# A graph network and mixture-of-experts kernel on one core: the edge units' first product gets a contraction of 128 rows, the experts' inner features six near-equal pieces

## The reference, cut to what matters

```
hid = silu(edge_length_embedded @ fc_w0 / sqrt(8))      # 8 features -> 64
w = hid @ fc_w1 / sqrt(64)                              # 64 -> 4 x 64 weights of one edge
msg = products of w with h[edge_src] and the edge's 4 attributes
y = segment_sum(msg, edge_dst)
```

```
h = silu(x @ w1[e].T) * (x @ w3[e].T)                   # 256 -> 682
out += gate[e] * (h @ w2[e].T)                          # 682 -> 256
```

## Time and profile before

| what | us |
|---|---|
| median of the runs shown | 4059.72 |
| span of the profiled execution | 4057.3 |
| edge convolution, from its barrier to its node products | 2790.9 to 3432.3 |
| node products and routing | 3432.3 to 3586.5 |
| routed experts, blocks | 3586.5 to about 4021 |
| sum of pairs and store of the output | to 4057.3 |

### The profile page before, as it was taken

One profiled execution on the slowest core, in us unless ns is written; L12 is line 12 of the kernel. 1 busy time (PEld: TensorE's weight loads), 2 busy tenths in 40 slices (PEclk: granted clock), 3 DMA queues, 4 the chain that ended last, 5 costly groups with the idle time before them and its releaser, 6 DMA issues. The chain is left out here.

```text
span 4057.3 us, 61050 instructions
## 1 busy us (share of the span) xinstructions
PE 3711.8 (91%) x18981; PEld 3087.0 (76%) x18981; DVE 2525.8 (62%) x5060; ACT 1533.3 (38%) x3578; POOL 758.0 (19%) x614
## 2 busy tenths in 40 slices
PE   5996879999999999999998799787999999779996
PEld 2554459989899899898997688655888888758884
DVE  7774755555555555555554555544777777577775
ACT  0363211121211211212112544334888886135553
POOL 0000000000000000000000200003888885012221
PEclk9997989999999999999999899898999999779998
DMA  1364112222222222222221211012333332411113
GB/s 41 64 102 87 48 50 78 87 67 85 76 79 86 74 80 87 67 85 76 79 85 40 66 30 31 13 41 61 93 93 93 94 93 68 177 44 35 38 35 116
DMA packets 297743, 288.61 MB, mean 71 GB/s; under 512 B 101485, under 2 KB 272847, under 8 KB 296806
## 3 DMA queue, kind: packets, MB, share of 16 engines
q1 hardware_dynamic: 233867, 208.29, 17.8%
q0 software_dynamic: 56576, 66.41, 6.4%
q10 hardware_dynamic: 7002, 10.15, 0.7%
HBM read 241.89 MB, written 42.47 MB: 70 GB/s over the span
## 5 line engine op out<-in xcount | busy, mean ns | idle before, releaser
L974 PE MATMUL bank<-a_wide,parts 125*128 125x448 f32 x4200 | 871.5, 367 | 0.1
L974 PEld LDWEIGHTS bank<-a_wide,parts 125*128 125x128 f32 x4200 | 785.7, 188 | 77.2 <-issue 10.1
L2205 POOL DMA_INDIRECT rows<-h_dram,src_t x400 | 493.5, 1234 | 124.1 <-DVE prod L2394 87.3
L2321 ACT ACTIVATE hot<-eq,ea 125x80 f32<-125x80 f32 x1600 | 413.2, 350 | 0.0
L949 POOL TENSOR_TENSOR nf_g<-nf,nf_g 128x896 fp32r<-128x896 f32 x42 | 94.5, 2249 | 1525.4 <-ACT nf_g L1112 1525.4
L1024 DVE CAST a_wide<-a_cols 125x2240 fp32r<-125x2240 bf16 x210 | 274.5, 1324 | 156.5 <-PE bank L974 141.0
L983 PE MATMUL bank<-nf_g,whh 128*128 128x448 f32 x1512 | 339.6, 369 | 0.0
L983 PE MATMUL bank<-msg,wc 128*128 128x448 f32 x1512 | 338.9, 368 | 0.0
L2247 PEld LDWEIGHTS bank<-prod,hot 125*80 125x80 f32 x2400 | 294.6, 150 | 54.1 <-issue 0.7
L2247 PE MATMUL bank<-prod,hot 125*80 125x128 f32 x2400 | 327.9, 273 | 0.0
L1117 ACT ACTIVATE msg<-bank 128x448 fp32r<-128x448 f32 x84 | 41.1, 542 | 702.6 <-PE bank L974 702.6
(11 more groups left out here) (431 smaller groups left out, 5894.4 us busy)
## 6 DMA issues: line engine op xcount, KB each, us to landing
a_cols<-a_dram SPq DMA_DIRECT2D x210, 546.9 KB
a_dram<-a_cols SPq DMA_DIRECT2D x15, 1250.0 KB, 10.9
w<-in_w SPq DMA_DIRECT2D x4, 2728.0 KB
deg_bc<-deg_dram SPq DMA_DIRECT2D x42, 224.0 KB, 6.1
gate_bc<-gate_dram SPq DMA_DIRECT2D x42, 224.0 KB, 3.2
rows<-h_dram,src_t POOLq DMA_INDIRECT x400, 4.2
w<-y_rows SPq DMA_DIRECT2D x12, 512.0 KB, 10.1
w<-in_w SPq DMA_DIRECT2D x5, 1024.0 KB
```

The source lines that it names most:

```text
L974: ins = nc.tensor.matmul(p_msg[f][:, 0:GW], parts[0:SPB, m, c * HB + k, f * 128:(f + 1) * 128], a_wide[u % 2][0:SPB, k, :], start=(c == 0 ...
L2205: nc.gpsimd.indirect_dma_start(out=rows[n % ITC][:, :], out_offset=None, in_=h_dram, in_offset=bass.IndirectOffsetOnAxis(ap=src_t[:, n:n + ...
L2321: ins = nc.scalar.activation(hot[:, q % 2, j, m, :], eq[:, q % 2, j, :], ACT.Copy, scale=ea4[:, q * UC + j, m:m + 1])
```

## The change

`ea8` and `fw0` get 128 partitions in place of 24. POOL fills both with zeros once, ahead of the zeros of `acc`; the loads of `ea8` still write 24 rows, and the product L2224 reads all 128. SP waits for the zeros ahead of its first load, DVE ahead of its first write to `fw0`. The 682 inner features are cut into four pieces of 114 and two of 113. The list of pieces also sets the loads of `w2`, the turns, the copies and the products down. DVE's two copies in `turned` become one.

```diff
-HCH = [(k * 128, min(128, HID1 - k * 128)) for k in range((HID1 + 127) // 128)]
+LONG, SHORT = (4, 114), (2, 113)
+HCH = [(k * LONG[1], LONG[1]) for k in range(LONG[0])] + [(LONG[0] * LONG[1] + k * SHORT[1], SHORT[1]) for k in range(SHORT[0])]
...
-        ea8 = sb(ctx, "ea8", [24, 2, UE], F32R)
+        ea8 = sb(ctx, "ea8", [128, 2, UE], F32R)
...
-        fw0 = sb(ctx, "fw0", [24, 128], F32R)
+        fw0 = sb(ctx, "fw0", [128, 128], F32R)
...
+                sp.wait_ge(rest_zero, START + 2)
                 with sp.Fori(0, rounds) as r:
...
-                        sp.dma_start(ea8[:, b, :].bitcast(F32), ea8_dram[:, q * UE:(q + 1) * UE]).then_inc(ea_in[b], 16)
+                        sp.dma_start(ea8[0:24, b, :].bitcast(F32), ea8_dram[:, q * UE:(q + 1) * UE]).then_inc(ea_in[b], 16)
...
             def _(pool):
+                nc.gpsimd.memset(fw0[:, :].bitcast(F32), 0.0).then_inc(rest_zero, 1)
+                nc.gpsimd.memset(ea8[:, :, :].bitcast(F32), 0.0).then_inc(rest_zero, 1)
                 nc.gpsimd.memset(acc[:, :, :], 0.0).then_inc(acc_zero, 1)
...
                 dve.wait_ge(w_split, START + 2)
+                dve.wait_ge(rest_zero, START + 2)
...
-                nc.vector.tensor_tensor(fw0[:, :], fw0_raw[:, :], fw0_high[:, :], ALU.subtract).then_inc(w_split, 1)
+                nc.vector.tensor_tensor(fw0[0:24, :], fw0_raw[:, :], fw0_high[:, :], ALU.subtract).then_inc(w_split, 1)
...
-    IN_0 = 4
+    IN_0 = LONG[0]
...
-                    nc.scalar.activation(g_t[:, 0:IN_0, :], p_g[0][:, 0:IN_0 * 128].rearrange("p (h c) -> p h c", c=128), ACT.Copy)\
+                    nc.scalar.activation(g_t[0:LONG[1], 0:IN_0, :], p_g[0][0:LONG[1], 0:IN_0 * 128].rearrange("p (h c) -> p h c", c=128), ACT.Copy)\
...
-                    o, sz = HCH[-1]
-                    nc.vector.tensor_copy(g_t[:, IN_0:NH - 1, :], p_g[1][:, 0:(NH - 1 - IN_0) * 128].rearrange("p (h c) -> p h c", c=128))
-                    at_h = (NH - 1 - IN_0) * 128
-                    nc.vector.tensor_copy(g_t[0:sz, NH - 1, :], p_g[1][0:sz, at_h:at_h + 128]).then_inc(gt_done, 1)
+                    nc.vector.tensor_copy(g_t[0:SHORT[1], IN_0:NH, :], p_g[1][0:SHORT[1], 0:SHORT[0] * 128].rearrange("p (h c) -> p h c", c=128))\
+                      .then_inc(gt_done, 1)
```

More of the change, by code:

```diff
@@ L2121, in edge_convolution @@
     src_t, rel0, base_row, rounds_t, iota_w = tables
-    (w_in, w_split, silu_done, hid_high, scaled, acc_zero, tab, ea_in_a, ea_in_b, hid_mm, hid_done, w_mm, eq_done, hot_done, p_done, sum_mm, sum_copied, turned, added,
+    (w_in, w_split, silu_done, hid_high, scaled, rest_zero, acc_zero, tab, ea_in_a, ea_in_b, hid_mm, hid_done, w_mm, eq_done, hot_done, p_done, sum_mm, sum_copied, turned, added,
      u_mm, mix_mm, t_done, b_done, x_done, stat_done, passed, *gathered) = sems(*("c_" + s for s in (
-         "w_in w_split silu hid_high scaled acc_zero tab ea_in_a ea_in_b hid_mm hid w_mm eq hot prod sum_mm sum_copied turned added "
+         "w_in w_split silu hid_high scaled rest_zero acc_zero tab ea_in_a ea_in_b hid_mm hid w_mm eq hot prod sum_mm sum_copied turned added "
          "u_mm mix_mm t b x stat passed").split()),
```

## The result

The changed kernel takes 4134.9 us (median of 4 runs, 4130.7 to 4137.5), the kernel before 4059.4 beside it (4056.9 to 4059.7): 1.019 times, 95% interval 1.0175 to 1.0204. It is slower, as forecast, but by 75 us where 42 were forecast, and outside the range.

A forecast was written before the change was run, and what follows sets the result against it. PE was taken to bound the edge units and expert blocks, with POOL next in the edge units. Terms -19 (experts' pieces), -11 (edge units) and +72 (w2 loads) gave +42, a median of 4101.7 us, range 4078 to 4122.

The forecast's parts named there:

- step 2: Edge units: padded first product speeds PE, POOL's gathers become the bound; -11 us (-3 to -16).
- step 4: Loads of w2: 114 rows use six DMA engines, 113 rows one, delaying the experts; +72 us (+63 to +93).
- Step 1: Expert blocks: pieces of 114 and 113 rows save PE 0.34 us in each of 56 blocks; -19 us.
- The PE half: Edge units: padding removes 0.35 us without streaming per first product on PE, 35 us if PE stayed the bound.
- lag: End of the edge stage: less time from the last gather to the last sums; 5.8 us gained.
- Step 3: POOL's added zero fill: 1.0 to 1.2 us, hidden by the pause ahead of the ninth gather; nothing.
- The low bound: Loads of w2: at 24.6 GB/s an engine they take 100.6 us, +63.
- A: Loads of w2 spread over 16 engines all the same; 4030 us; chance 0.06.
- B: The two 113-row w2 loads go to different engines; +31 us, 4061 in all; chance 0.03.
- C: Edge units: POOL is no bound, so they give -35 us; 4078; chance 0.06.
- D: Edge units and expert blocks: short products cost nothing in themselves, no gain; +72 us, 4132; chance 0.02.

The follow-up runs named there:

- e16: Whole change with the w2 loads cut at 112 rows, against the kernel before: 4070.0 us, ratio 1.0025.
- e9: Whole change with cut w2 loads and DVE's subtraction moved behind the third products, against the kernel before: 4030.5 us, ratio 0.9929.
- e10: As e9 but with the edge units' first product not padded (24 rows), against the kernel before: 4040.8 us, ratio 0.9955.
- e18: The kernel of e9 again, on the chip of e16, against the kernel before: 4029.1 us, ratio 0.9922.
- e11: Whole change with cut w2 loads and the hidden rows left in their PSUM bank, against the kernel before: 4028.5 us, ratio 0.9923.

## Why the prediction was right or wrong

*What bounds the kernel* was read rightly for PE, and POOL was named as the next in line. e16 confirms that: PE at 93%, POOL back to back.

The medians differ by 75.5 us where 42 were forecast, 33.5 more: +39.1 from step 2, -6.9 from step 4, -2.6 from the edge units' barrier, which came earlier, and +3.9 because the profiled run lies that far below the median.

*Step 1, the experts' pieces:* -19 forecast, -19.0 measured, by the same 0.34 us a block.

*Step 2, the edge units:* this is the step that failed, in sign: -11 forecast (-3 to -16), +28.1 measured. The PE half of it was right: the 0.35 us of each first product went. So was the landing of the gathers as DVE's release, with 5.3 us of lag gained where 5.8 were forecast. What failed are the words "I have no row for the collision in the new phase [...]; I take the middle". The middle lay between long gathers as they are (1.31) and none, as though the worst that a new phase could bring were the old one. It brought 1.71 in 82 of 100 units, 0.50 us over a plain gather instead of 0.10. Two things were at hand. First, rows 4's long gather was put down to the cast that runs beside it. The timeline that gives the law above, `eq` ending at 3153.97 and the gather at 3155.06, lay in the profile of before; a gather held until the end of an operation in flight can be held for as long as the longest of them, 0.68 us for the subtraction. That gives an upper bound of 1.09 + 0.68 = 1.77 for such a gather, 0.46 us more than now. With one a unit it is +46 us for 100 units, less the 5.8 of the lag, about +40. With that end the range would have held the result. Second, the change moves the bound from PE to POOL, and so the phase; a step that does so needs the price of every phase. e9 and e10 show that without the long gathers the padding is worth 10.3 us. That this is the forecast's -11 so nearly is partly luck: for gathers without any collision the working gave -14.8, and in e9 shorter collisions stay (mean gather 1.221 us, 1.211 without).

*Step 3, the zeros:* 1.1 us on POOL, hidden ahead of the ninth gather as forecast: it starts 26.2 us after the barrier, 26.1 before (at 2814.4 instead of 2817.0, since the barrier itself came 2.6 us earlier).

*Step 4, the loads:* +72 forecast, +65.1 measured. Six engines and one, as worked out from the divisors. The size was 10% off because one engine moved 23 to 25 GB/s in place of the 22.6 taken from `a_cols`. The low bound, +63 at 24.6 GB/s, was nearer. In DMA: Bandwidth & Descriptors, section Why a DMA increments its semaphore by 16 and not by 1, the Trainium skill puts 127 partitions on one engine; 113, another prime, behaves so too.

*The rivals:* A (spread over 16 engines) and B (two engines for the 113-row loads) are refuted by the 24 GB/s of the stretch, the rate of a single engine (six moved 138). C (POOL no bound) is refuted by PE's 93%, with gathers still 0.31 us apart. D (short products cost nothing) is refuted by the 0.34 us that the experts' blocks gained. None of them was the one that came. The miss was a term with too narrow bounds. The forecast's own terms reached up to 4134, and the range was then given as 4122; the measured 4134.9 lies above both.

The Trainium skill, SBUF — State Buffer, section SBUF: two separate sides, tells of a port pair that VectorE and GpSimd share, and names operations with two SBUF inputs as blocking a GpSimd operation that reads SBUF. The traces agree for subtraction and comparison. It also says that the pair is held for the whole instruction; this the measurement contradicts: a subtraction that begins 0.07 to 1.3 us into a gather isn't slowed (0.68 us throughout) and doesn't lengthen it. A comparison that begins 0.05 to 0.2 us into a gather can (up to 1.34 us).

## What to carry to other kernels

When a change shifts the bound from one engine to another, it shifts the phase between all of them: look for operations that exclude each other and price each phase, not just the one that the profile shows. An engine's gain is kept only if what takes over is undisturbed, and one instruction moved behind its neighbour can be enough (e18: 41 us against e16; with e11 the best of the versions here, 0.992 of the kernel before). Count rows of a transfer for divisors before rows of a contraction for balance: 114 and 113 rows cost 65 us in loads and gave 19 in products, and the loads cut at 112 rows keep the gain without the price.

## What the runs showed of the hardware

- A POOL gather that starts while DVE runs an operation with only SBUF operands ends 1.087 us after that operation (1476 of 1498 cases within 0.012), and otherwise takes 1.21; with one operand in PSUM there is no delay (118 cases of cast and subtraction).
- A DVE cast from SBUF to SBUF that begins 0.6 to 1.0 us into a gather ends 1.43 us after the gather's start. The same cast from PSUM takes 0.67 us instead of 0.41 and is never held.
- A load of 113 rows uses one DMA engine, 23 to 25 GB/s; one of 114 uses six (share 0.41, 138 GB/s); 112 rows and the rest apart bring the old time back.
- The kernel before takes 4059 us in three of the six sets of runs and 4085 to 4090 in three, with the difference in the edge stage (641 against 672). Each set ran on another chip, and the traces of the longer ones also hold fewer of the signals between engines, so chip and set can't be told apart. Waits there of up to 3.4 us for products whose records have ended stay unexplained.
